# The first layer's opening in another order: the first batch multiplied ahead of the second's statistics, and each later turn inside the query products before it

## The reference, cut to what matters

```python
ada = silu(c) @ w_adaln + b_adaln
shift, scale, gate, ... = split(ada, 6)
h = (x - mean) * rsqrt(var + eps)          # per token
h = h * (1 + scale) + shift                # per channel and batch
q, k, v = split(h @ w_qkv + b_qkv, 3)      # 288 -> 864, 16 heads of 18
o = softmax(q k^T / sqrt(18)) v            # per batch and head
x = x + gate * (o @ w_proj + b_proj)
```

## Time and profile before

| | us |
|---|---|
| median of 3 runs | 1669.87 |
| lowest and highest | 1662.98, 1670.25 |
| profiled execution | 1675.76 |
| its span in the profile | 1673.9 |
| PE busy | 1516.3 (91%) |
| DVE busy | 1247.6 (75%) |
| ACT busy | 979.7 (59%) |
| POOL busy | 770.1 (46%) |
| first q products of layer 0 | at 29.65 |
| first attention matmul of layer 0 | at 115.02 |

### The profile page before, as it was taken

The page is one execution under the profiler, slowest core; times in us unless marked ns, Lnnn a source line. Parts: engine busy times, 40 slices in busy tenths (PEclk is TensorE's granted clock), DMA queues, the critical chain, the costliest instruction groups (busy, mean ns, idle before and its releaser), DMA issues.

```text
span 1673.9 us, 28935 instructions
## 1 busy us (share of the span) xinstructions
PE 1516.3 (91%) x8965; PEld 973.0 (58%) x8965; DVE 1247.6 (75%) x2303; ACT 979.7 (59%) x1750; POOL 770.1 (46%) x1666
## 2 busy tenths in 40 slices
PE   5879999876999999896799998899998999989998
PEld 4632223665899988885522223788873222358875
DVE  7788887755789777667588886677878888675653
ACT  4647777541656654565467777444654777664432
POOL 0556640144475543015366666676766666560000
PEclk9999999977999999998899999999998999999999
DMA  6473324053955544325533343201055333400001
GB/s 171 114 204 70 91 73 112 15 43 59 262 142 147 156 138 124 113 84 166 168 75 88 78 104 58 45 4 19 4 139 141 83 76 89 101 3 1 1 1 57
DMA packets 111990, 151.38 MB, mean 90 GB/s; under 512 B 36596, under 2 KB 91878, under 8 KB 111739
## 3 DMA queue, kind: packets, MB, share of 16 engines
q1 hardware_dynamic: 105340, 135.04, 27.9%
q0 software_dynamic: 6528, 14.85, 8.7%
HBM read 113.40 MB, written 32.03 MB: 87 GB/s over the span
## 4 chain that ended last, share of the span: by engine, by line
PE 64%; DVE 19%; ACT 5%; issue 4%; DMA 3%; SPq 3%; another core or an unknown queue 1%; DVEq 0%; ACTq 0%
PE psum L1443 19%; PE psum L1588 9%; PE psum L1577 9%; PE psum L1563 8%; PE psum L1745 7%; PE psum L1882 5%; DVE minus_max L2211 2%; PE psum L1500 2%; DVE bn L2119 1%; DMA k_stack<-qk_parts_d 1%; DVE x_norm L2141 1%; ACT x_mod L1282 1%; SPq L802 1%; PE psum L1627 1%; DVE qk_r L2196 1%
## 5 line engine op out<-in xcount | busy, mean ns | idle before, releaser
L2211 DVE TENSOR_REDUCE minus_max<-psum 128x2 bf16<-128x1024 f32 x384 | 453.0, 1220 | 79.1 <-PE psum L1563 72.0
L1344 ACT ACTIVATE probs<-psum 128x512 f32<-128x512 f32 x768 | 418.1, 600 | 151.6 <-PE psum L1577 149.4
L1577 PE MATMUL psum<-q_stack,k_stack 109*128 109x512 bf16 x768 | 261.1, 387 | 7.5 <-ACT probs L1344 5.3
L1443 PE MATMUL psum<-x_split,w_hi 128*128 128x512 f32 (+1 forms) x684 | 244.6, 401 | 13.6 <-DVE x_tail L2158 4.7
L1563 PE MATMUL psum<-k_stack,q_stack 108*128 108x512 bf16 x720 | 222.0, 390 | 11.6 <-DVE minus_max L2211 8.5
L944 POOL TENSOR_TENSOR qr_m<-qr_m 64x8 f32<-64x8 f32 (+35 forms) x544 | 197.9, 364 | 42.6
L1577 PEld LDWEIGHTS psum<-q_stack,k_stack 109*128 109x128 bf16 x768 | 72.7, 98 | 245.4 <-ACT probs L1344 179.6
L1588 PE MATMUL psum<-probs,v_stage 128*32 128x512 f32 x1536 | 203.9, 604 | 1.1 <-ACT o_t L1333 1.1
L939 POOL TENSOR_TENSOR qr_m<-qr_rows 64x288 f32<-64x288 f32 (+31 forms) x64 | 45.7, 714 | 243.3 <-DMA qr_rows<-qr_rows 243.3
L1443 PEld LDWEIGHTS psum<-x_split,w_hi 128*128 128x128 f32 x684 | 129.9, 192 | 39.2 <-issue 11.3
L1443 PE MATMUL psum<-x_split,w_lo 128*128 128x512 f32 (+1 forms) x342 | 132.4, 387 | 0.0
(11 more groups left out here) (415 smaller groups left out, 3321.0 us busy)
## 6 DMA issues: line engine op xcount, KB each, us to landing
qk_parts_d<-qk_parts SPq DMA_DIRECT2D x36, 384.0 KB, 4.3
raw_b<-in_L_cond_w SPq DMA_DIRECT2D x30, 432.0 KB, 4.7
raw_a<-in_L_cond_w SPq DMA_DIRECT2D x30, 384.0 KB
q_stack<-qk_parts_d SPq DMA_DIRECT2D x48, 216.0 KB
k_stack<-qk_parts_d SPq DMA_DIRECT2D x48, 216.0 KB
q_stack<-qk_parts_d SPq DMA_DIRECT2D x48, 144.0 KB
k_stack<-qk_parts_d SPq DMA_DIRECT2D x48, 144.0 KB
moe_out_d<-branch SPq DMA_DIRECT2D x9, 576.0 KB, 3.5
```

The lines of the kernel that those rows point to most:

```text
L1344: act.activation(PE_[:, v // 4, v % 4, :], psum[:, score_bank(v), :], ACT.Exp, scale=SCALE).then_inc(s_e, 1)
L1443: i = pe.matmul(dst, a, r, start=(n == 0), stop=(n == len(terms) - 1))
L1577: pe.matmul(psum[:, score_bank(v), :], K6[0:STK + 1, g % 4, h, P * kt:P * kt + P], Q6[0:STK + 1, g % 4, h, :], start=True, stop=True).then ...
L2211: dve.tensor_reduce(MX[:, g % 2, 2 * u:2 * u + 2], psum[:, o:o + 2, :], AX.X, ALU.max, negate=True).then_inc(s_mx, 1)
```

## The change

- DVE makes only batch 0's statistics and norm ahead of the modulation's columns. Batch 1's statistics follow the low parts of the weights; its norm stands in `qkv(0)` in front of group 1's rest, and its `low` behind the copy of `qr_rows` and the statistics of batch 2.
- Batch 2's norm stands in `qkv(1)` in front of group 1, and the statistics of batch 3 in front of group 4. `low(2)` follows `qkv(1)`. Batch 3's norm stands in `qkv(2)` in front of group 0, and `low(3)` and the projection's low part follow the whole of `qkv(2)`.
- PE turns batch 0 alone ahead of `qkv(0)`. Batch 1 is turned inside `qkv(0)` behind group 3, batch 2 inside `qkv(1)` behind group 3, batch 3 inside `qkv(2)` behind group 2.
- ACT splits only the first third of the weights ahead of `turned(0)`, and the other two behind it. `turned(b + 1)` stands in `qk_parts(b)` in front of group 4 (batches 0 and 1) or group 3 (batch 2).
- No instruction is added or removed.

```diff
@@ ACT, qk_parts @@
                         turned(l, 0, 3, (0, 1) if m == 3 else (2,))
+                    if l == 0 and b < B - 1 and m == (QN - 1 if b < 2 else 3):
+                        turned(l, 0, b + 1)
                     if m == QN - 1 and b < B - 1:
                         values(l, b, (0, 1))
@@ ACT, main @@
                 if l == 0:
-                    for w in range(3):
-                        split_hi_qkv(l, w)
+                    split_hi_qkv(l, 0)
                     act.wait_ge(s_mc_, 1)
                     turned(l, 0, 0)
-                    turned(l, 0, 1)
+                    split_hi_qkv(l, 1)
+                    split_hi_qkv(l, 2)
                     mod_row(0)
                     qk_parts(l, 0)
-                    turned(l, 0, 2)
                     mod_row(1)
                     qk_parts(l, 1)
-                    turned(l, 0, 3)
                     split_hi("p", l, RAWP, WPH, WPT, s_rb, RB["p", l])
@@ PE, main @@
                     turn(l, 0, 0)
-                    turn(l, 0, 1)
-                    qkv(l, 0)
+                    qkv(l, 0, lambda n: turn(l, 0, 1) if n == 3 else None)
                     turn_p()
-                    turn(l, 0, 2)
                     mlp_mods()
-                    qkv(l, 1)
-                    turn(l, 0, 3)
+                    qkv(l, 1, lambda n: turn(l, 0, 2) if n == 3 else None)
@@ PE, last_turn @@
+                    if l == 0 and n == 2:
+                        turn(l, 0, 3)
@@ DVE, main @@
             first_stats(0)
-            first_stats(1)
             normalise(0, 0, 0)
-            normalise(0, 0, 1)
             first_mods()
...
                     split_lo_qkv(l, 1)
                     split_lo_qkv(l, 2)
+                    first_stats(1)
+                    qkv(l, 0, lambda m: normalise(l, 0, 1) if m == 1 else None)
+                    dve.wait_ge(s_pq, 1)
+                    dve.tensor_copy(QX[:, 0, :], psum[0:D3, 4, 0:C]).then_inc(s_pt, 1)
                     first_stats(2)
                     low(l, 0, 1)
-                    qkv(l, 0, lambda m: normalise(l, 0, 2) if m == KC else None)
-                    dve.wait_ge(s_pq, 1)
-                    dve.tensor_copy(QX[:, 0, :], psum[0:D3, 4, 0:C]).then_inc(s_pt, 1)
-                    first_stats(3)
+                    mlp_scale_rows()
+
+                    def third_rows(m):
+                        if m == 1:
+                            normalise(l, 0, 2)
+                        if m == QN - 1:
+                            first_stats(3)
+
+                    qkv(l, 1, third_rows)
                     low(l, 0, 2)
-                    mlp_scale_rows()
-                    normalise(l, 0, 3)
-                    qkv(l, 1)
+                    qkv(l, 2, lambda m: normalise(l, 0, 3) if m == 0 else None)
                     low(l, 0, 3)
                     split_lo(("p", l), RAWP, WPH, WPL, WPT)
-                    qkv(l, 2)
```

## The result

The changed kernel takes 1684.72 us, the median of 4 runs (1676.83 to 1688.52), beside 1666.59 for the kernel before in the same comparison (4 runs, 1662.98 to 1670.25; the prediction had three of them, with a median of 1669.87). The ratio is 1.0103, 95% interval 1.0056 to 1.0149, that is 9.3 to 24.8 us slower. The profiled execution has a span of 1675.1, only 1.2 over the profiled one of before (1673.9); why this pair shows so little is a question of its own, taken up behind the experiments.

A forecast was written before the change was run, and what follows sets the result against it. The opening's chain of waits up to the first attention matmul (115.02) was taken to set the span. A 5.6 us gain is lost in batch 0, the attention comes 9.8 later: 1669.87 + 9.8 = 1679.7 us, range 1671 to 1685.

The forecast's parts named there:

- part 4: SyncE's first stack load, released by `low(3)`, makes the first attention matmul 8.5 to 11.1 us later; 9.8 taken.
- Part 1: Opening up to batch 0's first products: they start at 24.05, not at 29.65, a gain of 5.6 us.
- Part 2: Batch 0: of the 5.6 us 0.5 is left, `low(1)` over at 50.1, or 51.8 if the clock falls.
- a clock that falls in the pause at chunk 2: Batch 0: after TensorE's 2.3 us pause, group 4 and two v tiles take about 1.7 us more.
- Part 3: Batches 1 and 2: 18.75 us each from first product to the next `low`'s end; `low(3)` over at 87.6 to 89.3.
- The cover for batch 3's statistics: VectorE's wait of some 5 us for the v copies hides them; without it they cost up to 4.2 us.
- the 115.02: Start in us of the first attention matmul in layer 0, in the profile of the kernel before.
- the prediction's own sign of being wrong: At the kernel's end: a span not longer by the shift at 115 us would show the prediction wrong.
- Rival A: Opening bound by TensorE: batch 1's products come 5.6 us sooner and the gain is kept, 1664.3 us; chance 0.07.
- Rival B: Before the attention: only the delay of TensorE's batch 3 products counts, the stacks have slack; 5 us, 1675; chance 0.13.
- Rival C: Attention's first round: something that doesn't move ends it and takes up the shift; no change, 1670; chance 0.06.
- Rival D: Clock falls in each batch and batch 3's stores crowd with the `raw_b` load: 13.2 us in all, 1683; chance 0.14.

The follow-up runs named there:

- `low(1)` experiment: Changed kernel with `low(1)` moved into batch 0's query products, ahead of group 4's rest and batch 2's statistics: ratio 1.0058 to the kernel before.
- kernel in which no batch waits: Changed kernel with VectorE's steps, the turns and the mods' products reordered: 1664.69 us, ratio 0.9964 to the kernel before; again 1665.34 us, ratio 0.9971.
- two `low(3)` experiments: Changed kernel with `low(3)` inside batch 2's products: ratio 1.0057; kernel before with `low(3)` and the projection weights' split behind batch 2's rests: 1675.35 us, ratio 1.0036.
- the stores ahead of the stack load: Changed kernel with the first stack load issued behind the store of batch 2's part 3 instead of part 0: ratio 1.0096 to the kernel before.

## Why the prediction was right, and where not

The forecast was 1679.7 (1671 to 1685), 9.8 us over the median of before, slower. Measured were 1684.72, then 1682.49; both in the range and above its middle, the first by only 0.3 us under its upper end. Against the kernel before in the same comparison the forecast's 9.8 us stand beside 17.2 and 13.5 by the ratios: the direction and the mechanism are right, the size is low. With part 4 put right it would be about 11. What the first comparison shows above that is within its interval (9.3 to 24.8), and that its median of four runs fell inside the range is in part luck.

- Part 1 (first products at 24.05, group 3 at 32.0): 24.16 and 32.34. Right.
- Part 2 (VectorE idle for over 4 us ahead of group 4's rest, `low(1)` over at 50.1 to 51.8, batch 1 at 50 to 52): idle 4.46, 50.62, 50.68. Right, and the `low(1)` experiment shows that this order is the cause. I leaned to a clock that falls in the pause at chunk 2 (1.7 us). In the profile after it didn't: granted clock 1.00 at 38 to 40. It did in others, see below, and cost 1.5 there (52.19 for 50.68).
- Part 3 (batch 2 at 69 to 71, `low(3)` over at 87.6 to 89.3): 70.02 and 88.78. Right: batches 1 and 2 took 19.3 and 18.8 for the 18.75 worked out. The cover for batch 3's statistics was just enough: they end at 66.36 and part 0 of group 4, which the rest waits for, at 66.16. The prediction put `low` at 1.95 each; it took 2.42 and 2.27 here, since its tail was longer.
- Part 4 (stack load right behind `low(3)`, part 0 waits for a landing part, attention at 123.6 to 126.1): 88.92, a wait of 4.08, attention 126.46. The mechanism is right and the last term was too small: from the stack load to the attention 37.54 us, where I had 35.96 to 36.8. Taking the middle gave 9.8 for what was 11.4. Both of my values come from single profiled stretches. In the twelve profiles in which the load keeps its place in the queue the stretch takes 36.66 to 38.35 us, and the 36.66 of the profile of before is the lowest of them. What makes it longer is open. In the profile after, two things stand out: the second set of stack loads held SyncE for 2.75 with its first DMA (0.83 before), and TensorE's granted clock was 0.50 at 102 to 104, among the early scores. In the second profile of the changed kernel the same DMA took 0.82 and the clock was 1.00 in that window, and the stretch was 37.76 all the same, so neither can be called the cause. That DMA in the two profiles of the changed kernel:

```profile
100.23 2.75 SPq L802 DMA_DIRECT2D q_stack<-qk_parts_d  x1
```

```profile
101.42 0.82 SPq L802 DMA_DIRECT2D q_stack<-qk_parts_d  x1
```

- "Whatever the change does to the 115.02 is what it does to the span": borne out by the table over a range of 19 us. In the first pair of profiles alone the prediction's own sign of being wrong was there, a span that is not longer by the shift (1.2 us for 11.4); the timed runs decide against it.
- Rival A (the gain is kept) was ruled out by the order and not by a limit of the engine: in the kernel in which no batch waits most of it is kept. Its condition, `low(1)` over by 45, is met there (43.93). Rival B fell with the two `low(3)` experiments. Rival C fell with all runs. Rival D (1683) has the size of the two medians. Its clock is not borne out: the cold start of each batch (0.50 at 52 to 54, 72 to 74 and 90 to 94) is in the forecast already, through the rows of layer 1, and behind the pauses inside batches 1 and 2 (1.34 and 1.00 us) the granted clock was 1.00. Its other half, stores that crowd with the `raw_b` load, could be what makes part 4 longer; no run tested it.

## What to carry to other kernels

When a step is moved in a hand-written order, look for the wait that counts it in another queue (here a load on SyncE that waits for the fourth `low`), and price the step by that queue's delay, not by its own length. A gain at the head of such a pipeline is kept only if the next items of every engine move with it: work the order out for all engines together, batch by batch, before you trust a gain in one.

## What the runs showed of the hardware

- The same pause, two clocks. Ten profiles hold the pause of 2.23 us at chunk 2 of batch 0 with the same instructions ahead of it. In the windows 38 to 40 the granted clock was 1.00 (2.4 GHz) in four of them and 0.50 to 0.65 (down to 1.2 GHz) in six. Two of the kernel in which no batch waits, the first and the second time:

```profile
38.00:40.00 2.00, 2.00 (x12) 1.43 (x11) 1.93 (x9) 1.94 (x4) 0.00 (x0) 1.00 0.91 306
```

```profile
38.00:40.00 2.00, 2.00 (x7) 1.05 (x6) 1.97 (x9) 1.97 (x4) 0.00 (x0) 0.54 0.89 305
```

A pause of that length can't be priced from one profile; 0 and 1.5 us are both right. The instructions ahead are the same, but not their clock: at 28 to 30, early in batch 0, it was 0.50 to 0.57 in the four profiles that later stayed at 1.00, and 0.91 to 1.00 in five of the six that fell; in the sixth (the stores ahead of the stack load) it was 0.50. Whether the one leads to the other was not tested.

- A tail of 32x512 on VectorE (`x_tail`) took 0.68 us at 23.42 with GpSimd idle, and 1.18 at 49.44 with GpSimd busy for all of 49.40 to 50.60. The Trainium skill ("SBUF — State Buffer", section "Who interferes with whom") says that a VectorE instruction with two inputs in SBUF contends with a GpSimd instruction that reads SBUF, through a shared read interface; by that rule the longer tail is expected, and this pair agrees. But it took 0.68 at 57.48 in the kernel in which no batch waits, with GpSimd busy for all of 57.50 to 58.20, so busy time alone doesn't tell. GpSimd's instructions were of 64x288 elements in the first case (49.28 and 50.05) and of 64x1 in the other (56.46 and 57.89); that the size decides was not tested.
- The landing of a stored part that others wait for took 4.08 us, beside 4.26 and 4.32 in the trace of before.
